# An adaLN block on one core: normalised rows of batches 2 and 3 turned by VectorE blocks and a DMA instead of TensorE

## The chip, the cores and the metric

The kernel runs on one core of a Trainium2 chip. The metric is the device time of one execution in microseconds (us). Engines are called PE (TensorE), DVE (VectorE), ACT (ScalarE), POOL (GpSimd) and SP (SyncE, which here only issues DMAs); PEld is the weight load of PE.

## The reference

Inputs are x (4 batches x 512 tokens x 512 features, fp32), a conditioning row c per batch, and weights. Cut to what matters:

```python
mod = (silu(c) @ wmod).reshape(4, 6, 1, 512)          # sa, ca, ga, sb, cb, gb
ga, gb = sign(g) * max(|g|, 0.25)                      # both gates
h = layernorm(x) * (1 + ca) + sa
qkv = h @ Wqkv + bqkv                                  # 512 -> 3 x 128
attn = softmax(q @ k.T / sqrt(128)) @ v
x = x + ga * (attn @ Wo + bo)
h = layernorm(x) * (1 + cb) + sb
logits = h @ gate_w.T + expert_bias                    # 4 experts, the best one counts
ffn = h @ W_up.T + (h @ A[e].T) @ B[e].T               # rank 8
out = x + gb * ffn
```

## The kernel before

All of x stays in SBUF (`xs`, 128 partitions = tokens of a tile, 4 batches x 4 tiles x 512). Every fp32 product is made of three products of a high and a low part (`products`, L344): `h1hi`/`h1lo`, `phi`/`plo`, `h2hi`/`h2lo` and so on. Each engine has an order written out by hand; semaphores counted per batch and tile tie the orders together, and no scheduler moves anything. PSUM's eight banks are given out by a list in order (`psum_plan`), and whoever opens a bank waits until its former holder is emptied.

A batch b goes through these steps. Layer norm 1: DVE statistics (`ln1_stats`, `ln1_moments`), POOL `ln1_deviation` and `ln1_offset` (1/std and shift), then ACT `ln1_normalise(b)` writes `xn1`, tokens on partitions. The projection needs features on partitions, so PE `x1_transposes(b)` turns 16 blocks of 128x128 into four banks; ACT `h1_high` evacuates them times (1 + ca), rounded, into `h1hi`; DVE `h1_low` makes `h1lo`. PE `qkv(b)` in two halves, `scores`, then DVE `maxima` and ACT `softmax`, PE `p_transposes`, ACT `pt_high` and DVE `pt_low`, PE `pv`, ACT `o_high` and DVE `o_low`, PE `out_projection`, DVE `residual` and `ln2_moments`, POOL `ln2_deviation`, ACT `ln2_normalise`, PE `x2_transposes`, ACT `h2_high` and DVE `h2_low`, and last the feed-forward products `up(b, t)` of 12 matmuls each, which PE runs between the attention steps of batch b + 1. DVE `gate_ffn` and POOL `outputs` finish a tile, SP stores it.

Names for the steps below: the loop `for b in range(1, B)` on every engine handles attention of batch b and the feed-forward part of b - 1. In it PE runs `x1_transposes(b + 1)` in the middle of `up(b - 1, 0)`. POOL runs `add_output_bias(b)`, then `output_weights(b + 1)` (L1379), which waits for `ga_bc`, a gate row of the next batch spread over the partitions, then `output_bias`, `ln1_deviation(b + 2)`, `ln1_offset(b + 2)` and `ln2_deviation(b, ...)` with `outputs(b - 1, ...)` between. SP issues in this order: `write_gate(1)` (waits for the gate rows "gb", which DVE's `gate_rows_evacuate` writes), the two spreads of gb, then the spread of `ga_bc` for batch 2, then the stores.

Of the kernel before, what the change touches and what calls it, by code (L numbers as in the profile page):

```python
# [11 lines left out]
P = 128  # L12
B = 4
# [12 lines left out]
BY_ACT = 3  # L26

# [16 lines left out]
def psum_plan():  # L44
# [43 lines left out]
def adaln_block(nc: bass.Bass, x, wqkv, bqkv, wo, bo, wup, gate_w, expert_bias, lora_a, lora_b, c, wmod, out):  # L88
    place, earlier = psum_plan()
    with ExitStack() as ctx:  # L90
# [3 lines left out]
        def sem(name):  # L94
# [11 lines left out]
        c_row = sb("c_row", [B, H])  # L106
# [58 lines left out]
        fb_hi = stage[:, 0, :]  # L165
# [21 lines left out]
        gates_out = sem("gates_out")  # L187
        stored = sem("stored")
# [10 lines left out]
            ln1_stats ln1_aggr ln1_var ln1_rstd ln1_shift xn1_ready xn1_by_act x1T_psum h1_hi h1_lo  # L199
# [57 lines left out]
        def _(sp):  # L257
# [25 lines left out]
            sp.dma_start(c_row[:], c).then_inc(c_in, 16)  # L283
# [48 lines left out]
        def _(pe):  # L332
# [296 lines left out]
            for kt in range(NK):  # L629
                mm = nc.tensor.transpose(dst[:, B * kt:B * kt + B], c_row[:, kt * P:(kt + 1) * P], ident[0:B, 0:B])  # L630
# [44 lines left out]
            for b in range(1, B):  # L675
# [60 lines left out]
        def _(act):  # L736
            def h1_high(b, kts=range(NK)):
                for kt in kts:
                    act.wait_ge(S["x1T_psum"], NK * b + kt + 1)
                    if b == 0 and kt % 2 == 0:  # L740
                        act.wait_ge(S["modT_ready"], 1 + kt // 2)
                    if b and kt == 0:
                        act.wait_ge(S["qkv_psum"], 3 * b)
# [172 lines left out]
            ln1_normalise(2)  # L916
            for b in range(1, B):
# [35 lines left out]
        def _(dve):  # L953
# [163 lines left out]
            def v_low(b):  # L1117
# [3 lines left out]
                                        ALU.subtract).then_inc(S["v_lo_ready"], 1)  # L1121

# [170 lines left out]
            for b in range(1, B):  # L1293
# [15 lines left out]
                if b + 2 < B:  # L1309
                    ln1_stats(b + 2, (0, 1, 2, 3))  # L1310
                    ln1_moments(b + 2)
                o_low(b)
                if not last:
# [7 lines left out]
                    qk_low(b + 1)  # L1321
                else:
# [25 lines left out]
        def _(pool):  # L1348
            def ln1_deviation(b):
# [95 lines left out]
            for b in range(1, B):  # L1445
# [8 lines left out]
                if not last:  # L1454
                    ln2_deviation(b, (0, 1))
# [32 lines left out]
```

## Time and profile before

| what | us |
|---|---|
| median of 3 runs (lowest to highest) | 194.16 (193.78 to 194.17) |
| the profiled execution, its own time | 194.07 |
| its span, first to last instruction | 192.2 |
| PE busy in the span | 177.0 (92%) |
| DVE, ACT, POOL busy | 137.6, 90.9, 79.5 |

The span is 1.9 us shorter than the execution's time. Times in rows count from the start of the span. Busy time of matmuls overlaps: a matmul of 512 columns is shown as some 0.39 us, but one starts every 0.23 us.

### The profile page before, as it was taken

Reading aid. Unit: us, or ns where it says so; the run is one execution under the profiler, and the core shown is the slowest. Engines: PE = TensorE matmul, PEld = TensorE weight load, DVE = VectorE, ACT = ScalarE, POOL = GpSimd, SP = SyncE. Lnnn points to the kernel's source line nnn. Section 1 sums busy time; section 2 is a strip of 40 time slices with the busy share of each in tenths; the row PEclk is TensorE's granted clock in tenths of the full one; section 3 lists DMA queues with packets and bytes.
Section 4 is the critical chain, followed back from the end, with each engine's and each line's share of the span. In section 5 each row is a group of like instructions: output and inputs, shape, how many; then the busy total and the mean of one; then the engine's idle time right before and its main releaser. Section 6 shows DMA issues by size and latency. Waiting matters only on the chain.

```text
span 192.2 us, 2846 instructions
## 1 busy us (share of the span) xinstructions
PE 177.0 (92%) x951; PEld 139.0 (72%) x951; DVE 137.6 (72%) x339; ACT 90.9 (47%) x172; POOL 79.5 (41%) x106
## 2 busy tenths in 40 slices
PE   6897999989998789986999999999999999988991
PEld 6874757866766658864888788878887887767770
DVE  1839748799989854796885478569566493986964
ACT  3355045954168976420746596113565622456110
POOL 3544200278154980005778940015696000332750
PEclk9999999999999999999999999999999999999999
DMA  5999996910033000022021500000232000001315
GB/s 173 381 385 386 382 269 108 398 64 5 0 79 141 3 2 0 0 76 95 0 109 55 164 3 0 0 0 3 109 122 42 3 0 3 0 0 55 144 42 196
DMA packets 12221, 19.21 MB, mean 100 GB/s; under 512 B 2812, under 2 KB 3328, under 8 KB 12208
## 3 DMA queue, kind: packets, MB, share of 16 engines
q1 hardware_dynamic: 12208, 19.05, 29.2%
q8 instruction: 7, 0.11, 0.2%
q14 instruction: 6, 0.05, 0.1%
HBM read 14.83 MB, written 4.21 MB: 99 GB/s over the span
## 4 chain that ended last, share of the span: by engine, by line
PE 45%; DVE 4%; issue 1%; ACT 1%; POOL 1%; DVEq 0%; POOLq 0%
PE bank L349 31%; PE bank L476 2%; PE bank L503 2%; PE bank L579 1%; DVE xs L1152 1%; DVE stats L1159 1%; PE bank L527 1%; PE bank L529 1%; PE bank L461 1%; PE bank L455 1%; PE bank L458 1%; PE bank L432 1%; PE bank L557 1%; DVE f_gb L1217 1%; ACT h2hi L844 1%
## 5 line engine op out<-in xcount | busy, mean ns | idle before, releaser
L1402 POOL TENSOR_TENSOR rstd<-var_eps,neg_half 128x1 f32<-128x1 f32 x16 | 8.8, 553 | 47.3 <-DVE var_eps L1163 47.3
L349 PE MATMUL bank<-wup_lo,h2hi 128*128 128x512 f32 x64 | 26.7, 417 | 0.6 <-DVE lbw L1085 0.6
L825 ACT ACTIVATE xn_p<-xs,shift,rstd 128x512 f32<-128x512 f32 x16 | 12.9, 815 | 27.7 <-POOL shift L1405 27.7
L349 PE MATMUL bank<-wup_hi,h2hi 128*128 128x512 f32 x64 | 25.3, 395 | 0.0
L349 PE MATMUL bank<-wup_hi,h2lo 128*128 128x512 f32 x64 | 25.2, 393 | 0.0
L1417 POOL TENSOR_TENSOR xs<-xs,f_gb 128x512 f32<-128x512 f32 x14 | 17.9, 1292 | 7.2 <-DVE f_gb L1217 7.2
L349 PE MATMUL bank<-h1lo,wqkv_hi 128*128 128x512 f32 x48 | 19.7, 411 | 1.2 <-ACT wqkv_hi L818 1.2
L1394 POOL TENSOR_TENSOR xs<-xs,gabo 128x512 f32<-128x512 f32 x16 | 20.3, 1302 | 0.1
L349 PE MATMUL bank<-h1hi,wqkv_hi 128*128 128x512 f32 x48 | 19.0, 395 | 0.0
L349 PE MATMUL bank<-h1hi,wqkv_lo 128*128 128x512 f32 x48 | 18.9, 394 | 0.0
L1379 POOL TENSOR_TENSOR wo_ga<-wo_raw,ga_bc 128x512 f32<-128x512 f32 x4 | 5.1, 1280 | 32.2 <-DMA ga_bc<-gates_dram 17.3
L1152 DVE SCALAR_TENSOR_TENSOR xs<-bank,row_inv,xs 128x512 f32<-128x512 f32 x16 | 12.0, 747 | 4.0 <-PE bank L349 2.6
L1126 DVE TENSOR_REDUCE row_max<-bank 128x1 f32<-128x512 f32 x16 | 10.9, 684 | 4.8 <-PE bank L461 4.8
L349 PEld LDWEIGHTS bank<-wup_lo,h2hi 128*128 128x128 f32 x64 | 12.1, 188 | 3.0 <-DVE lbw L1085 1.0
L349 PEld LDWEIGHTS bank<-wup_hi,h2hi 128*128 128x128 f32 x64 | 12.0, 188 | 2.8
L349 PEld LDWEIGHTS bank<-wup_hi,h2lo 128*128 128x128 f32 x64 | 12.1, 189 | 2.0
L1091 DVE SCALAR_TENSOR_TENSOR h1lo<-bank,modT_ca,h1hi 128x512 fp32r<-128x512 f32 x16 | 11.1, 742 | 3.4 <-ACT h1hi L744 3.3
L1135 DVE TENSOR_TENSOR plo<-bank,phi 128x512 fp32r<-128x512 f32 x16 | 10.0, 685 | 3.5 <-ACT phi L796 3.5
L961 DVE BATCH_NORM_STATS2 stats<-xs 128x6 f32<-128x512 f32 x16 | 10.2, 679 | 3.2 <-DMA xs<-in_L_attn_x_dram 3.2
L788 ACT ACTIVATE xn_p<-bank,neg_max 128x512 f32<-128x512 f32 x16 | 11.0, 686 | 3.0 <-DVE neg_max L1128 3.0
L1217 DVE TENSOR_TENSOR f_gb<-bank,gb_bc 128x512 f32<-128x512 f32 x16 | 10.6, 687 | 2.3 <-PE bank L579 2.1
L349 PEld LDWEIGHTS bank<-h1lo,wqkv_hi 128*128 128x128 f32 x48 | 9.0, 188 | 4.0 <-ACT wqkv_hi L818 1.4
(180 smaller groups left out, 421.7 us busy)
## 6 DMA issues: line engine op xcount, KB each, us to landing
out_dram<-xs SPq DMA_DIRECT2D x16, 256.0 KB, 2.0
stage<-in_L_wmod_dram SPq DMA_DIRECT2D x3, 1024.0 KB, 6.8
xs<-in_L_wmod_dram SPq DMA_DIRECT2D x3, 1024.0 KB, 9.0
xs<-in_L_attn_x_dram SPq DMA_DIRECT2D x3, 1024.0 KB, 6.7
xs<-in_L_attn_x_dram SPq DMA_DIRECT2D x2, 512.0 KB, 3.9
f_gb<-in_L_ffn_W_up_dram SPq DMA_DIRECT2D x1, 1024.0 KB, 10.5
gb_bc<-gates_dram SPq DMA_DIRECT2D x4, 256.0 KB, 3.6
xn_p<-in_L_attn_Wqkv_dram SPq DMA_DIRECT2D x4, 192.0 KB, 7.9
```

The source lines that it names most:

```text
L349: mm = nc.tensor.matmul(dst, w, m, start=first and i == 0, stop=last and i == total - 1)
L788: nc.scalar.activation(xn2_p[:, t, :], at("S", b, t)[:], ACT.Exp, bias=neg_max[:, t:t + 1], scale=SCORE_SCALE, accum_out=row_sum[:, t:t + ...
L825: nc.scalar.activation(xn2_p[:, t, :], xs[:, b, t, :], ACT.Identity, bias=shift[:, 1, t:t + 1], scale=rstd[:, 1, t:t + 1]).then_inc(S["xn2 ...
L961: nc.vector.bn_stats(stats[:, 0, t, :], xs[:, b, t, :]).then_inc(S["ln1_stats"], 1)
L1091: nc.vector.scalar_tensor_tensor(h1lo[:, kt, :], at("x1T", b, kt)[:], modT["ca"][:, kt, b:b + 1], h1hi[:, kt, :].bitcast(F32), ALU.mult, A ...
L1126: nc.vector.reduce_max(row_max[:, t:t + 1], at("S", b, t)[:], AX_X).then_inc(S["max_ready"], 1)
L1135: nc.vector.tensor_tensor(plo[:, :, q], at("PT", b, t)[:].rearrange("p (k q) -> p k q", k=NT), phi[:, :, q].bitcast(F32), ALU.subtract).th ...
L1152: nc.vector.scalar_tensor_tensor(xs[:, b, t, :], at("Y", b, t)[:], row_inv[:, t:t + 1], xs[:, b, t, :], ALU.mult, ALU.add).then_inc(S["x2_ ...
L1217: nc.vector.tensor_tensor(f_gb[:, n % 4, :], at("F", b, t)[:], gb_bc[:, b % 2, :], ALU.mult).then_inc(S["f_gb_ready"], 1)
L1394: nc.gpsimd.tensor_tensor(xs[:, b, t, :], xs[:, b, t, :], gabo[:], ALU.add).then_inc(S["xb_ready"], 1)
L1402: nc.gpsimd.tensor_tensor(rstd[:, 1, t:t + 1], var_eps[:, 1, t:t + 1], neg_half[:, 0:1], ALU.pow).then_inc(S["ln2_rstd"], 1)
L1417: nc.gpsimd.tensor_tensor(xs[:, b, t, :], xs[:, b, t, :], f_gb[:, n % 4, :], ALU.add).then_inc(S["out_ready"], 1)
```

## The change

For batches 2 and 3 PE no longer turns the normalised rows. ACT writes `xn1` in blocks of 32 features; DVE turns every 32x32 block in place (`turn_blocks`, four instructions); SP moves 16 pieces of 32 partitions x 2 KB from `xn1` to `stage` (`move_turned`), so that features stand on partitions; ACT scales them in place by (1 + ca) (`x1_scale`, four instructions) and rounds them into `h1hi` (`h1_high`, four); POOL makes `h1lo` (`h1_low`, four). The orders of all engines are written anew around that. `fb_hi` moves from `stage` to `c_rows`, and the banks of `fb` and `gzb` are exchanged. `NB` is 4, `BLOCK` 32, `TURNED` 2.

```diff
 # SP
+def move_turned(b):
+    sp.wait_ge(S["xn1_turned"], NT * (b - TURNED + 1))
+    if b > max(TURNED, 2):
+        sp.wait_ge(S["h1_lo"], NK * b)
+    for a in range(NB):
+        for c in range(NB):
+            sp.dma_start(turned_in[b][a * BLOCK:(a + 1) * BLOCK, c],
+                         xn1_blocks[c * BLOCK:(c + 1) * BLOCK, a]).then_inc(turned_moved, 16)
 ...
+            move_turned(2)
             write_gate(1)
 ...
                 if b + 2 < B:
                     spread_gate(0, b + 2)
+                if b == 1:
+                    move_turned(3)
 # PE
-                if last:
-                    up(b - 1, 0)
-                else:
-                    up(b - 1, 0, (0, 1))
-                    x1_transposes(b + 1)
-                    up(b - 1, 0, (2, 3))
+                up(b - 1, 0)
                 z_to_tokens(b - 1)
+                up(b - 1, 1, (0,))
                 p_transposes(b)
-                up(b - 1, 1)
+                up(b - 1, 1, (1, 2, 3))
 # ACT
+def x1_scale(b):
+    act.wait_ge(turned_moved, 16 * NB * NB * (b - TURNED + 1))
+    for kt in range(NK):
+        nc.scalar.activation(turned_in[b][:, :, kt], turned_in[b][:, :, kt], ACT.Copy,
+                             scale=modT["ca"][:, kt, b:b + 1]).then_inc(S["x1_scaled"], 1)
 ...
-            ln1_normalise(2)
             for b in range(1, B):
 ...
                 if b == 1:
+                    ln1_normalise(2)
+                    gz_evacuate(0)
 ...
+                if b == 2:
+                    x1_scale(3)
+                pt_high(b)
+                if b == 1:
+                    x1_scale(2)
                 if not last:
                     h1_high(b + 1)
-                pt_high(b)
                 o_high(b)
 # DVE
+def turn_blocks(b):
+    for t in range(NT):
+        xn1_done(dve, b, t + 1)
+        nc.vector.transpose(xn1_blocks[:, :, :, t], xn1_blocks[:, :, :, t]).then_inc(S["xn1_turned"], 1)
 ...
                 if b == 1:
+                    gate_shift()
+                    turn_blocks(2)
                     ffn_shift_rows()
-                    gate_shift()
-                if not last:
-                    h1_low(b + 1)
+                    ln1_stats(3, (0, 1, 2, 3))
+                    ln1_moments(3)
+                pt_low(b)
                 if b == 1:
                     gate_columns("gb")
-                pt_low(b)
+                choose_expert(b - 1)
                 if b == 1:
                     gate_rows_evacuate("gb")
-                choose_expert(b - 1)
                 inverse_sums(b)
-                if b + 2 < B:
-                    ln1_stats(b + 2, (0, 1, 2, 3))
-                    ln1_moments(b + 2)
                 o_low(b)
 ...
                     qk_low(b + 1)
+                    if b == 1:
+                        turn_blocks(3)
 # POOL
+def h1_low(b):
+    for kt in range(NK):
+        pool.wait_ge(S["h1_hi"], NK * b + kt + 1)
+        nc.gpsimd.tensor_tensor(by_blocks(h1lo[:, kt, :]), turned_columns(b, kt),
+                                by_blocks(h1hi[:, kt, :].bitcast(F32)), ALU.subtract).then_inc(S["h1_lo"], 1)
 ...
                     ln1_offset(b + 2)
                 if not last:
+                    h1_low(b + 1)
                     ln2_deviation(b, (0, 1))
```

Where POOL's order stood in pass b = 1 of the loop before (`wo_ga` is `output_weights(2)`, `var_eps` to `rstd` of 128x1 is `ln2_deviation`):

```order
L1379 TENSOR_TENSOR wo_ga<-wo_raw,ga_bc 128x512 [waits wo_lo_ready,wo_hi_ready,ga_bc_in0]
L1384 TENSOR_TENSOR gabo<-bo_bc,ga_bc 128x512 [waits xb_ready]
L1351 TENSOR_TENSOR rstd<-var_eps,neg_half 128x4 [waits ln1_var]
L1367 TENSOR_SCALAR shift<-moments,rstd 128x1 [waits ln1_rstd]
L1367 TENSOR_SCALAR shift<-moments,rstd 128x1 x3
L1402 TENSOR_TENSOR rstd<-var_eps,neg_half 128x1 [waits xn2_ready,ln2_var]
```

And the same place now:

```order
L1443 TENSOR_TENSOR wo_ga<-wo_raw,ga_bc 128x512 [waits wo_lo_ready,wo_hi_ready,ga_bc_in0]
L1448 TENSOR_TENSOR gabo<-bo_bc,ga_bc 128x512 [waits xb_ready]
L1415 TENSOR_TENSOR rstd<-var_eps,neg_half 128x4 [waits ln1_var]
L1431 TENSOR_SCALAR shift<-moments,rstd 128x1 [waits ln1_rstd]
L1431 TENSOR_SCALAR shift<-moments,rstd 128x1 x3
L1410 TENSOR_TENSOR h1lo<-stage,h1hi 128x512 [waits h1_hi] x4
L1466 TENSOR_TENSOR rstd<-var_eps,neg_half 128x1 [waits xn2_ready,ln2_var]
```

Four subtractions that DVE did before now stand on POOL between the shifts of layer norm 1 and the deviations of layer norm 2.

ACT's order now, pass b = 2, after the scores of batch 2 (`phi` is `pt_high(2)`, `stage` is `x1_scale(3)`, `h1hi` is `h1_high(3)`):

```order
L832 ACTIVATE xn_p,row_sum<-bank,neg_max 128x512 [waits negmax_ready]
L788 ACTIVATE stage<-stage,modT_ca 128x4x128 [waits turned_moved]
L788 ACTIVATE stage<-stage,modT_ca 128x4x128 x3
L840 ACTIVATE phi<-bank 128x4x128 [waits O_psum,PT_psum]
L840 ACTIVATE phi<-bank 128x4x128 [waits PT_psum] x3
L776 ACTIVATE h1hi<-stage 128x512 [waits x1_scaled,qkv_psum]
```

The wait for the 16 DMAs of batch 3 stands ahead of `pt_high(2)`; before, `h1_high(3)` stood there, and it waited for PE.

## Rows read from the trace of the kernel before

**Rows 1.** The page, part 1: busy time of each engine.
```profile
PE 177.0 (92%) x951; PEld 139.0 (72%) x951; DVE 137.6 (72%) x339; ACT 90.9 (47%) x172; POOL 79.5 (41%) x106
```

**Rows 2.** Timeline of PE: start, us, engine, line, op, count, [idle before].
```profile
73.30 1.91 PE L432 MATMUL bank<-ident,xn 128*128 128x128 f32 x16
74.97 0.47 PE L349 MATMUL bank<-wup_lo,h2hi 128*128 128x512 f32 x1
...
89.02 0.47 PE L349 MATMUL bank<-wo_lo,o_hi 128*128 128x512 f32 x1 [1.76 <-DVE o_lo L1144]
...
101.18 1.91 PE L503 MATMUL bank<-ident,xn_p 128*128 128x128 f32 x16
...
121.45 0.39 PE L349 MATMUL bank<-plo,v_hi 128*128 128x512 f32 x1
```

**Rows 3.** Timeline of POOL, end of the prelude and pass b = 1.
```profile
66.13 5.06 POOL L1394 TENSOR_TENSOR xs<-xs,gabo 128x512 f32<-128x512 f32 x4
88.53 1.28 POOL L1379 TENSOR_TENSOR wo_ga<-wo_raw,ga_bc 128x512 f32<-128x512 f32 x1 [17.34 <-DMA ga_bc<-gates_dram]
...
93.07 0.56 POOL L1402 TENSOR_TENSOR rstd<-var_eps,neg_half 128x1 f32<-128x1 f32 x1
...
97.01 0.55 POOL L1402 TENSOR_TENSOR rstd<-var_eps,neg_half 128x1 f32<-128x1 f32 x1
97.89 1.29 POOL L1417 TENSOR_TENSOR xs<-xs,f_gb 128x512 f32<-128x512 f32 x1
```

**Rows 4.** Timeline of ACT.
```profile
64.26 2.93 ACT L813 ACTIVATE xn<-xs,shift,rstd 128x512 f32<-128x512 f32 x4
...
69.55 0.68 ACT L788 ACTIVATE xn_p<-bank,neg_max 128x512 f32<-128x512 f32 x1
...
100.09 0.82 ACT L825 ACTIVATE xn_p<-xs,shift,rstd 128x512 f32<-128x512 f32 x1 [1.31 <-POOL shift L1405]
...
117.54 2.07 ACT L796 ACTIVATE phi<-bank 128x512 fp32r<-128x512 f32 x4 [0.96 <-PE bank L476]
```

**Rows 5.** Timeline of DVE.
```profile
77.96 2.48 DVE L1135 TENSOR_TENSOR plo<-bank,phi 128x512 fp32r<-128x512 f32 x4
81.87 0.68 DVE L1059 COPY gates<-bank 4x512 f32<-4x512 f32 x1 [1.43 <-PE bank L386]
...
85.09 2.44 DVE L961 BATCH_NORM_STATS2 stats<-xs 128x6 f32<-128x512 f32 x4
...
87.92 0.68 DVE L1144 TENSOR_TENSOR o_lo<-bank,o_hi 128x512 fp32r<-128x512 f32 x1
...
106.63 1.46 DVE L1113 SCALAR_TENSOR_TENSOR qk_lo<-bank,qb,qk_hi 128x512 fp32r<-128x512 f32 x2 [1.36 <-ACT qk_hi L766]
```

**Rows 6.** Groups by line: us busy, mean ns of one.
```profile
L1274 DVE COPY xn<-lora_b_raw 128x128 f32<-128x128 f32 x3 | 3.7, 1295 | 0.0
...
L851 ACT ACTIVATE wo_hi<-wo_ga 128x512 fp32r<-128x512 f32 x4 | 2.5, 630 | 0.4 <-POOL wo_ga L1379 0.4
```

**Rows 7.** Line L326, the stores: ns min/median/max of an issue; us to landing.
```profile
L326 SPq DMA_DIRECT2D out_dram<-xs x16: 332/332/338, 97.1 to 189.8; - x16
...
DMA to landing us min/median/max: 2.0/2.0/2.1
```

**Rows 8.** Line L281, the gate spreads, the same view.
```profile
DMA to landing us min/median/max: 3.1/3.6/3.9
```

**Rows 9.** Windows: stretch, length, busy of PE, PEld, DVE, ACT, POOL; granted clock; DMA.
```profile
190.00:191.60 1.60, 0.00 (x0) 0.00 (x0) 0.00 (x0) 0.00 (x0) 0.00 (x0) 1.00 0.45 168
191.60:192.20 0.60, 0.00 (x0) 0.00 (x0) 0.00 (x0) 0.00 (x0) 0.00 (x0) 0.55 0.00 0
```

**Rows 10.** Timeline of PE: its first matmuls and its last.
```profile
4.09 3.58 PE L335 MATMUL bank<-ident 128*128 128x128 f32 x16
...
13.44 1.06 PE L335 MATMUL bank<-ident 128*128 128x128 f32 x8
...
187.52 0.40 PE L579 MATMUL bank<-lbw,zT 128*128 128x512 f32 x1
```

More of the change, by code:

```diff
@@ L26 @@
 BY_ACT = 3
+TURNED = 2
+BLOCK = 32
+NB = P // BLOCK
 QUARTER = 32
@@ L57, in psum_plan @@
         (7, "x2T", 0, 0), (4, "x2T", 0, 1), (6, "x2T", 0, 2), (5, "x2T", 0, 3),
-        (2, "fb"), (7, "gzb"), (4, "gz", 0),
+        (7, "fb"), (2, "gzb"), (4, "gz", 0),
     ]
@@ L66, in psum_plan @@
         order += [(f[0], "F", b - 1, 0)]
-        if not last:
-            order += [(m[kt], "x1T", b + 1, kt) for kt in range(NK)]
         order += [(m[4], "zl", b - 1)] + [(m[t], "PT", b, t) for t in range(NT)] + [(f[1], "F", b - 1, 1)]
@@ L105, in adaln_block @@
         gz_bias = sb("gz_bias", [2 * GZ, B])
-        c_row = sb("c_row", [B, H])
+        c_rows = sb("c_rows", [P, H])
         silu_tmp = sb("silu_tmp", [P, 3, NK * B])
@@ L164, in adaln_block @@
         lora_b_rep = xn1[:, 0, 0:NK * ZROWS].rearrange("p (k a z) -> p k a z", k=NK, a=3)
-        fb_hi = stage[:, 0, :]
+        fb_hi = c_rows
+        xn1_blocks = xn1[:].rearrange("p t h -> p (t h)").rearrange("p (a k t i) -> p a k t i", a=NB, k=NK, t=NT)
+        turned_in = {b: (stage if b > 1 else h2lo)[:].bitcast(F32).rearrange("p t h -> p (t h)").rearrange(
+            "p (c k t i) -> p c k t i", c=NB, k=NK, t=NT) for b in range(TURNED, B)}
         mod_rows = gb_bc
@@ L187, in adaln_block @@
         gates_out = sem("gates_out")
+        turned_moved = sem("turned_moved")
         stored = sem("stored")
@@ L237, in tiles_of, with turned_columns, by_blocks, xn1_free @@
             return range(2 * half[0], 2 * half[0] + 2) if half else range(NT)
+        def turned_columns(b, kt):
+            return turned_in[b][:, :, kt].rearrange("p c t i -> p t c i")
+        def by_blocks(columns):
+            return columns.rearrange("p (t c i) -> p t c i", t=NT, c=NB)
+        def xn1_free(engine, b):
+            if b <= TURNED:
+                engine.wait_ge(S["x1T_psum"], NK * b)
+            else:
+                engine.wait_ge(turned_moved, 16 * NB * NB * (b - TURNED))
         def xn1_done(engine, b, t=NT):
@@ L629, in _ @@
             for kt in range(NK):
-                mm = nc.tensor.transpose(dst[:, B * kt:B * kt + B], c_row[:, kt * P:(kt + 1) * P], ident[0:B, 0:B])
+                mm = nc.tensor.transpose(dst[:, B * kt:B * kt + B], c_rows[0:B, kt * P:(kt + 1) * P], ident[0:B, 0:B])
             mm.then_inc(S["cT_psum"], 1)
@@ L738, in h1_high @@
                 for kt in kts:
+                    if b and kt == 0:
+                        act.wait_ge(S["qkv_psum"], 3 * b)
+                    if b >= TURNED:
+                        act.wait_ge(S["x1_scaled"], NK * (b - TURNED) + kt + 1)
+                        nc.scalar.activation(by_blocks(h1hi[:, kt, :]), turned_columns(b, kt),
+                                             ACT.Copy).then_inc(S["h1_hi"], 1)
+                        continue
                     act.wait_ge(S["x1T_psum"], NK * b + kt + 1)
@@ L809, in ln1_normalise @@
                     if t == 0:
-                        act.wait_ge(S["x1T_psum"], NK * b)
+                        xn1_free(act, b)
                         if b == 2:
                             act.wait_ge(S["loraB_psum"], 1)
-                    nc.scalar.activation(xn1[:, t, :], xs[:, b, t, :], ACT.Identity, bias=shift[:, 0, t:t + 1],
+                    nc.scalar.activation(xn1_blocks[:, :, :, t].rearrange("p a k i -> p k a i"),
+                                         xs[:, b, t, :].rearrange("p (k a i) -> p k a i", k=NK, a=NB), ACT.Identity, bias=shift[:, 0, t:t + 1],
                                          scale=rstd[:, 0, t:t + 1]).then_inc(S["xn1_by_act"], 1)
@@ L1090, in h1_low @@
                     dve.wait_ge(S["h1_hi"], NK * b + kt + 1)
+                    if b >= TURNED:
+                        nc.vector.tensor_tensor(by_blocks(h1lo[:, kt, :]), turned_columns(b, kt),
+                                                by_blocks(h1hi[:, kt, :].bitcast(F32)), ALU.subtract).then_inc(S["h1_lo"], 1)
+                        continue
                     nc.vector.scalar_tensor_tensor(h1lo[:, kt, :], at("x1T", b, kt)[:], modT["ca"][:, kt, b:b + 1],
@@ L1321, in _ @@
                     qk_low(b + 1)
+                    if b == 1:
+                        turn_blocks(3)
                 else:
```

12 lines of the change are left out of this document (4 added, 8 removed).

## The prediction

> **What bounds the kernel now.** I read the page first: PE is busy 92% of the span [rows 1]. Then PE's timeline: one matmul of 512 columns starts every 0.23 us almost without a gap, so in the middle of the program PE is the bound, and work taken from it counts in full only as long as nothing else becomes the last to arrive. So I read, for the two passes that change (attention of batch 1 and of batch 2), when each other engine delivers. The reader is to see two things. First, PE reaches `x2_transposes(1)` at 101.18 [rows 2], and ACT's last normalised tile for it, begun at 100.09, ends at 100.91 [rows 4]: there is 0.27 us of slack, and behind that tile stands a chain of POOL that starts at 88.53, when the gate row `ga_bc` of batch 2 has landed [rows 3]. POOL is 41% busy over the span, yet here it is as late as PE. Second, PE reaches `pv(2)` at 121.45 [rows 2], 20.27 after 101.18; that is all the room that ACT and DVE have there; ACT's last part for it is ready at 119.61 (117.54 + 2.07) [rows 4], DVE's 0.7 later.
>
> **What the change takes from PE.** Two times 16 transposes. The next matmul starts 1.67 us after the first of them [rows 2], so 3.3 us in all. In pass 1 it also takes away most of the largest wait, 1.76 us for `o_lo` [rows 2]: DVE ran the statistics of batch 3 just before it (85.09 to 87.92) [rows 5], and these now stand ahead of `pt_low(1)`. With all of this PE would end some 5 us earlier. The rest is whether it can.
>
> **Pass 1, the gate row.** SP issues the spread of `ga_bc` behind `write_gate(1)`, which waits for DVE's copy of the gate rows "gb". I follow DVE.
> - ACT's normalisation of batch 2 (2.93 us) [rows 4] now stands behind `softmax(1)`. Softmax ended at 70.23 (69.55 + 0.68) [rows 4]; without the normalisation ahead of it I take it 0.8 earlier, paced by the maxima: 69.4. Normalisation ends at 72.4.
> - DVE turns tile by tile behind it. No row shows a block transpose. Nearest are plain passes over 512 columns at 0.61 us each (2.44 for four) [rows 5]; above, the slowest SBUF copy took 1.3 us [rows 6]. Below 0.61 nothing is gained here, since ACT delivers a tile only every 0.7. I take 0.61 to 0.65: the last ends at 73.05.
> - ACT evacuates `gz` and `fb`, two copies of 0.6 like its other copies [rows 6], to 73.6; `ffn_shift_rows`, a pass of 0.7 with a semaphore on either side, to 74.4; statistics and moments of batch 3, 2.83 [rows 5], to 77.25; `pt_low(1)`, 2.48 [rows 5], to 79.75. It began at 77.96 before and begins 0.7 earlier now.
> - `gate_columns`, four tiny instructions, 0.65 as an estimate, then `choose_expert(0)`, 2.5 (between the copy's end and 85.09) [rows 5], which now stands ahead of the copy; the copy 0.68 [rows 5]. It ends at 83.7, against 82.55 (81.87 + 0.68) before.
> - From the copy's end to POOL's start two DMAs and their issues take 88.53 - 82.55 = 5.98 [rows 3, 5]. So POOL starts `output_weights(2)` at 89.7, 1.15 later than before. The 16 DMAs of batch 2, issued ahead of `write_gate(1)` from 73.1 on, are done by then (below).
>
> **Pass 1, POOL.** `output_weights(2)` to `ln1_offset(3)`: 93.07 - 88.53 = 4.54 [rows 3], to 94.24. Then the four subtractions of `h1_low(2)`: a two-input pass of POOL costs 5.06 us for four, one every 1.25 [rows 3], so 5.0, to 99.25. Before, DVE did them and POOL was already waited for. Then `ln2_deviation(1)` for four tiles at 0.88 each, with two `outputs` at 1.25 between (97.01 to 97.89, and 1.29 overlapped) [rows 3]: 6.05, to 105.3. ACT's normalisation 0.82 [rows 4], and 0.14 to PE: `x2_transposes(1)` starts at 106.3 against 101.18, **5.1 us late**. PE has nothing else to run: `qkv(2)`'s first half waits for the first two `h1_low` parts (95.5 and 96.8) and is over at 99.7, so PE stands still for about 6.6 us. All gains of pass 1, the transposes and the `o_lo` wait, fall into this gap. Whatever holds `o_high(1)` back behind the scaling on ACT falls into it too, up to some 5 us.
>
> **The clock in that gap.** PE's granted clock stays at 2.4 GHz through the longest wait of the middle, 1.76 us. After its last matmul (over at 187.92) [rows 10] it holds to 191.6 and is lower in the next window, a mean of 0.55 of full, which means 1.2 GHz [rows 9]: 3.7 us of rest were enough there, and 6.6 are expected here. I take it to fall. What that costs: the 16 warm-up matmuls at the program's start came one every 0.21 us ((3.58 - 0.4) / 15), eight of the same kind at 13.44 one every 0.11 [rows 10]. So each us of work at the low level loses half of itself. At the start at least these 3.58 us ran at the low level, a loss of 1.8, and twice as long would be 3.6. Taken: 2.5; zero if the clock holds.
> The Trainium skill, "TensorE: Matmul & The Clock Gate", HAM oscillation, has the rule that a long enough gap between bursts throttles PE again and the next burst begins cold. The end of this trace agrees; by the rule the sum has the 2.5, without it it has not.
>
> **Pass 2, the DMAs.** Count from x2_transposes(1), called X. DVE ends `qk_low(2)` at X + 6.9 (106.63 + 1.46) [rows 5]. `turn_blocks(3)` follows with 4 x 0.6, to X + 9.3. SP issues 16 DMAs: an issue takes 0.332 [rows 7] and the next follows 0.04 later, so 15 x 0.37 = 5.6, and the last lands 2.0 after its issue as a store does [rows 7]: X + 16.9. Bounds: 0.3 a piece and, since no row shows a landing in SBUF from SBUF, three quarters of the store's 2.0 (6.0 in all); 0.5 a piece and 3.6 as a gate spread [rows 8] (11.1); taken 7.6, since stores are plain copies issued by the same engine. ACT has x1_scale(3) **ahead of** `pt_high(2)`: 4 x 0.6 (0.630 for a copy from SBUF [rows 6]) to X + 19.3, `pt_high` 2.07 [rows 4] to X + 21.4, DVE's last `pt_low` 0.7 later: pv(2) starts at X + 22.1, against X + 20.27 before: **1.9 us late**, with bounds 0.3 and 5.4. PE's saving of pass 2, 1.67, is lost in this wait as well. Behind it `h1_high(3)` (2.2) and `o_high(2)` fit under pv's 2.8, and POOL's `h1_low(3)` (5.0, from X + 22 on) ends before the first deviation of batch 2 is asked for at about X + 29. From there on the rest of the program is as before; pass 3 only gets `p_transposes` 0.7 later in PE's order, with 2.1 us of matmuls between them and `pv(3)` for ACT and DVE.
>
> **The sum.** 194.07 + 5.1 + 2.5 + 1.9 = **203.6 us**. That is against the profiled execution; its time lies 0.09 under the median of 194.16, which I leave out.
>
> **The rivals.**
> - The clock holds at 2.4 GHz in the gap (the activity before it or the phase saves it): 201.1. Against it stands only the end of this trace. 20%.
> - DVE's block transposes are slow, 1.3 us each. For it: the copies of `xn1` from SBUF took that beside POOL's work [rows 6]. Pass 1 then ends the turning at 70.1 + 5.2 = 75.3 rather than 73.05 and `ffn_shift_rows` at 76.1 rather than 74.4, so +1.7; in pass 2 +2.8: 208.1. Against it: these copies had pieces of 32 columns at odd places and ran beside POOL, which waits in pass 1. 12%. The Trainium skill, "VectorE: DVE Perf Modes", The three transpose paths, gives 311 ns for 128 columns of bf16; an estimate of four times that is 1.24 us for 512, which would make this rival's time by the page. No row here shows it.
> - The DMAs are slow as at the upper bound, or PE's second gap (3.5 us before pv(2)) lets the clock fall a second time: 206 to 207. 13%.
> - PE stays the bound, because POOL gets `ga_bc` and finishes `h1_low(2)` early. Place: POOL's chain to `ln2_deviation(1)`. It decides if POOL reaches this by 94 rather than 99.25; then PE is never held, and 194.07 - 3.3 - 1.8 = 189 us, faster. For it: POOL is idle from 71.2 to 88.53. Against it: it is idle because it waits for `ga_bc` (17.34) [rows 3], the change puts `choose_expert(0)` ahead of that copy, and POOL's order is fixed. 4%; half-way cases that end near before, 3%.
> The forecast itself has the remaining 48%.
>
> **Range and chances.** Low end: clock holds and the DMAs at their lower bound, 194.07 + 5.1 + 0.3 = 199.5. High end: forecast with slow transposes or the DMAs' upper bound, 208. What is left out below and above is about 2 in 10. A difference under 0.2% (0.4 us) can't be told from none here. Faster 0.05, same 0.02, slower 0.93.
>
> **What would show it.** In the profile after: POOL's `wo_ga` starts near 89.7, its four `h1lo` rows follow at 94.2 with 1.25 each, PE's `x2` transposes of batch 1 start near 106.3 with an idle of about 6 us before them released by ACT's normalisation, and matmuls behind it come at 0.43 us for some 5 us. PE waits 3 to 4 us before pv(2), released by DVE `plo`, behind ACT `stage` waiting for a DMA. The chain that ended last goes through POOL and through 16 SBUF-to-SBUF DMAs. Wrong would be: `wo_ga` before 88, `h1lo` rows well under 1 us, or no idle of PE before x2 of batch 1. The four bn_stats of batch 3 ahead of `pt_low(1)` should leave no `o_lo` wait of DVE's making.

## The result and the profile after

The changed kernel takes **208.31 us** (median of 4 runs, 207.67 to 208.68) against 194.08 for the kernel before on the same chip: ratio 1.0732, 95% interval 1.0703 to 1.0762. The direction was right; the time lies 4.7 above the forecast and 0.3 above the range. The profiled run took 208.41, its span 206.7, 14.5 more than before.

The page, part 1 and one row of part 2, then one row of part 4 (the chain that ended last, by line):

```profile
PE 178.8 (86%) x919; PEld 139.2 (67%) x919; DVE 138.8 (67%) x339; ACT 95.5 (46%) x180; POOL 89.4 (43%) x114
...
PEclk9999999999999999976999998569999999999999
...
PE bank L386 25%; SPq L314 9%; POOL h1lo L1410 2%; DVE xn L1179 2%; PE bank L540 2%; DMA ga_bc<-gates_dram 2%; POOL rstd L1466 2%; DVE qk_lo L1166 1%; DVE h2lo L1151 1%; POOL xs L1481 1%; DVE plo L1193 1%; DVE xs L1210 1%; DVE stats L1217 1%; PE bank L498 1%; DMA stage<-xn 1%
```

PE issues 32 matmuls fewer than in [rows 1] and is still busy 1.8 us longer. The two dips of its clock row account for it: the 21 matmuls of 512 columns in them are shown as 0.63 us instead of 0.39. And a queue that before was no part of the chain, SP issuing the pieces (L314), is now 9% of it. PE's timeline, to be held against [rows 2]:

```profile
91.25 0.77 PE L386 MATMUL bank<-wo_lo,o_hi 128*128 128x512 f32 x1 [5.48 <-DVE o_lo L1202]
91.81 0.63 PE L386 MATMUL bank<-wo_hi,o_lo 128*128 128x512 f32 x1
...
106.35 1.97 PE L540 MATMUL bank<-ident,xn_p 128*128 128x128 f32 x16 [0.24 <-ACT xn_p L870]
...
133.82 0.76 PE L386 MATMUL bank<-plo,v_hi 128*128 128x512 f32 x1 [8.62 <-DVE plo L1193]
134.38 0.63 PE L386 MATMUL bank<-phi,v_lo 128*128 128x512 f32 x1
```

PE stands still twice: 5.48 us before `out_projection(1)`, where it had waited 1.76, and 8.62 before `pv(2)`, where it had not waited. X, the start of `x2_transposes(1)`, is at 106.35 instead of 101.18 (+5.17), and `pv(2)` at X + 27.47 instead of X + 20.27 (+7.20). Behind both gaps a matmul of 512 columns is followed by the next after 0.43 us instead of 0.23. Windows (stretch, length, busy of PE, PEld, DVE, ACT, POOL, granted clock, share and GB/s of the DMA engines) show why:

```profile
86.00:91.00 5.00, 0.00 (x0) 0.00 (x0) 0.69 (x1) 4.75 (x9) 1.06 (x1) 0.90 0.44 157
91.00:97.00 6.00, 5.75 (x14) 4.61 (x15) 1.78 (x4) 2.93 (x4) 5.90 (x10) 0.51 0.01 3
97.00:106.00 9.00, 9.00 (x40) 7.04 (x38) 7.57 (x16) 2.96 (x4) 8.06 (x12) 1.00 0.14 52
...
125.00:127.00 2.00, 0.21 (x1) 0.00 (x0) 0.00 (x0) 0.00 (x0) 0.00 (x0) 1.00 0.43 103
127.00:134.00 7.00, 0.18 (x1) 0.21 (x2) 2.81 (x5) 5.88 (x11) 0.79 (x1) 0.54 0.04 10
134.00:138.00 4.00, 4.00 (x10) 3.13 (x11) 2.47 (x12) 0.68 (x2) 4.00 (x4) 0.52 0.00 0
138.00:150.00 12.00, 12.00 (x55) 9.64 (x55) 8.61 (x18) 3.50 (x5) 4.68 (x9) 1.00 0.06 22
```

PE rests, the clock falls to 1.2 GHz during the rest, and it stays there for the first stretch of work behind it (0.51 and 0.52 of full). In the first rest it falls only near the end (a mean of 0.90 from 86 to 91), in the second early (0.54 from 127 on). The other engines (ACT, then POOL, then SP's queue, then DVE's new operation):

```profile
85.15 2.56 ACT L788 ACTIVATE stage<-stage,modT_ca 128x512 f32<-128x512 f32 x4 [7.26 <-DMA stage<-xn]
87.62 2.17 ACT L776 ACTIVATE h1hi<-stage 128x512 fp32r<-128x512 f32 x4
89.69 0.57 ACT L848 ACTIVATE o_hi<-bank 128x512 fp32r<-128x512 f32 x1
...
128.12 2.56 ACT L788 ACTIVATE stage<-stage,modT_ca 128x512 f32<-128x512 f32 x4 [8.09 <-DMA stage<-xn]
130.58 2.03 ACT L840 ACTIVATE phi<-bank 128x512 fp32r<-128x512 f32 x4
```

```profile
89.94 1.27 POOL L1443 TENSOR_TENSOR wo_ga<-wo_raw,ga_bc 128x512 f32<-128x512 f32 x1 [18.81 <-DMA ga_bc<-gates_dram]
...
94.44 4.99 POOL L1410 TENSOR_TENSOR h1lo<-stage,h1hi 128x512 fp32r<-128x512 f32 x4
...
105.19 0.27 POOL L1469 TENSOR_SCALAR shift<-moments,rstd 128x1 f32<-128x1 f32 x1
```

```profile
73.57 10.10 SPq L314 DMA_DIRECT2D stage<-xn  x16
...
115.76 10.89 SPq L314 DMA_DIRECT2D stage<-xn  x16
```

```profile
71.07 2.47 DVE L1179 STREAM_TRANSPOSE xn<-xn 128x512 f32<-128x512 f32 x4
```

Read together: DVE's turning costs 0.62 us a tile, as taken. Sixteen DMAs take SP 10.1 us to issue, and the data is ready for ACT at 85.15, 11.6 us after the last tile was turned (73.54). ACT's `o_high(1)` stands behind scaling and `h1_high(2)`, so it begins at 89.69 and PE waits for its low part. POOL, busy without a break from 89.94 to 105.46, arrives at x2_transposes(1) at the same time as PE. Its chain isn't independent of the pieces either. From the view of the chain that ended last (start, us, what), the last of batch 2's pieces, the write of the gate rows right behind it, and one piece of batch 3:

```profile
83.08 0.59 SPq L314
83.72 1.62 DMA gates_dram<-gates
...
122.02 1.46 SPq L314
```

`write_gate(1)` had to wait for DVE's copy of the gate rows, which ended at 83.55 (82.88 + 0.67), and for SP, which was busy with the pieces until 83.67. The two ends lie 0.1 us apart.

### The profile page after: what moved, and what is told of

It reads as the page before. It is cut to its first block, busy times and chain, and to the rows that moved or that the text cites. A ratio compares the mean times of both kernels' runs of the same rounds, so it can differ in the third digit from the quotient of the medians.

```text
span 206.7 us, 2829 instructions
## 1 busy us (share of the span) xinstructions
PE 178.8 (86%) x919; PEld 139.2 (67%) x919; DVE 138.8 (67%) x339; ACT 95.5 (46%) x180; POOL 89.4 (43%) x114
## 4 chain that ended last, share of the span: by engine, by line
PE 37%; DVE 12%; SPq 10%; POOL 8%; DMA 4%; issue 3%; ACT 3%; POOLq 0%; DVEq 0%
PE bank L386 25%; SPq L314 9%; POOL h1lo L1410 2%; DVE xn L1179 2%; PE bank L540 2%; DMA ga_bc<-gates_dram 2%; POOL rstd L1466 2%; DVE qk_lo L1166 1%; DVE h2lo L1151 1%; POOL xs L1481 1%; DVE plo L1193 1%; DVE xs L1210 1%; DVE stats L1217 1%; PE bank L498 1%; DMA stage<-xn 1%
## 5 line engine op out<-in xcount | busy, mean ns | idle before, releaser
L1410 POOL TENSOR_TENSOR h1lo<-stage,h1hi 128x512 fp32r<-128x512 f32 x8 | 10.0, 1280 | 14.5 <-ACT h1hi L776 14.5
L386 PE MATMUL bank<-plo,v_hi 128*128 128x512 f32 x16 | 7.4, 462 | 8.6 <-DVE plo L1193 8.6
L386 PE MATMUL bank<-wo_lo,o_hi 128*128 128x512 f32 x16 | 7.6, 476 | 6.0 <-DVE o_lo L1202 5.9
```

Of the source, the lines that this page charges most:

```text
L386: mm = nc.tensor.matmul(dst, w, m, start=first and i == 0, stop=last and i == total - 1)
L1410: nc.gpsimd.tensor_tensor(by_blocks(h1lo[:, kt, :]), turned_columns(b, kt), by_blocks(h1hi[:, kt, :].bitcast(F32)), ALU.subtract).then_inc ...
```

## The experiments

All times are medians. The kernel before was run beside them on the same chip each time: 193.69 (probe, few, low_dve, scale_late), 193.84 (warm, early, pool_half), 193.74 (warm32, best, moved) and 193.78 (best_sp). Beside the changed kernel it was 194.08, and the changed kernel itself was run only there, so a difference of two medians from different groups is uncertain by some 0.3 us. Times read from traces don't depend on that.

**probe: DMAs by themselves, behind the end of the kernel before.** One group of DMAs after another, with all engines idle; the group that copies as the change does, SBUF to SBUF, 32 partitions x 2 KB (L348 in its rows):

```diff
+for i in range(16):
+    sp.dma_start(probe_b[32 * (i // 4):32 * (i // 4) + 32, i % 4, :], probe_a[32 * (i % 4):32 * (i % 4) + 32, i // 4, :]).then_inc(probed, 16)
```

> The kernel before, with groups of DMAs issued by SP behind its last store, each group waited for: 16 stores of 128 partitions x 2 KB back to back; 16 stores of 32 partitions x 2 KB; 16 copies from SBUF to SBUF of 32 partitions x 2 KB, as the change makes them; 4 copies SBUF to SBUF of 128 partitions x 2 KB; 4 of 32 partitions x 8 KB; 4 of 32 partitions x 2 KB, each waited for before the next. It asks why an issue of the change takes 0.59 us where a store takes 0.33. Theory A, the form (SBUF at both ends): the third and the last groups show 0.59, both groups of stores 0.33. Theory B, back-to-back issue fills a queue: every group of 16 settles near 0.6 and the last group, issued alone, shows 0.33. Theory C, the number of partitions: groups with 32 partitions 0.59, those with 128 0.33. The time is some 40 to 60 us above the kernel before and means nothing by itself.

Rows of the view of one line (ns min/median/max of an issue, first and last start): 128-partition stores, 32-partition stores, pieces back to back, pieces each waited for:

```profile
L340 SPq DMA_DIRECT2D probe_dram<-wup_hi x16: 326/642/652, 191.6 to 200.9; - x16
```
```profile
L344 SPq DMA_DIRECT2D probe_dram<-wup_hi x16: 302/426/437, 204.0 to 211.2; - x16
```
```profile
L348 SPq DMA_DIRECT2D stage<-wup_hi x16: 586/591/617, 212.9 to 222.5; - x16
```
```profile
L360 SPq DMA_DIRECT2D stage<-wup_hi x4: 507/507/508, 236.1 to 242.0; - x4
```

The price follows both from the form and from the company. A store of 128 partitions takes 332 ns where stores come one by one [rows 7], and 326 as the first of the probe's group; the same store behind others takes 642. A store of 32 partitions behind others is 426, a copy of 32 partitions into SBUF 591, or 507 when each is waited for. One piece follows the other after (222.5 - 212.9) / 15 = 0.64 us on a quiet chip, as in the changed kernel. So the engines and the other DMAs that ran beside the pieces in the changed kernel don't make them slow. Two groups more had bigger copies into SBUF: 602 ns an issue and 2.5 us to landing for 128 partitions x 2 KB, 662 ns and 4.3 us for 32 partitions x 8 KB. Four issues of the second kind carry the bytes of sixteen pieces; no run here tries to merge the pieces into so few.

**few: 4 of the 16 pieces of each batch** (the other 12 blocks are not moved, so what ACT scales is partly old data; the work behind it is the same).

```diff
-                    for c in range(NB):
+                    for c in (a,):
 ...
```

> The changed kernel, but only 4 of the 16 pieces of each batch are moved (those with equal indices); the other 12 are left out, so batches 2 and 3 are computed from stale columns. Theory: SP's serial issue is what made pass 2 late. The move shrinks from 12.4 us to 4 x 0.63 + 2.0 = 4.5; ACT's scaling of batch 3 then starts at 120.3 instead of 128.1, pv(2) at 125.6 instead of 133.8, and PE's clock does not fall there: 208.3 - 8.2 - 1.9 = 198.2 us. In pass 1 the start of x2_transposes(1), 106.35, stays, as POOL's chain sets it. Rival, the landing of a copy into SBUF is what is slow and not its issue: 4 pieces take nearly as long as 16, 206 or more. Rival, both passes shrink: 193 or less.

Measured: **201.69** (ratio 1.0415, 1.0398 to 1.0433), 6.6 less than the changed kernel, 3.5 more than expected. PE's rows:

```profile
96.92 0.47 PE L386 MATMUL bank<-h1lo,wqkv_hi 128*128 128x512 f32 x1 [3.34 <-issue]
...
107.39 3.67 PE L540 MATMUL bank<-ident,xn_p 128*128 128x128 f32 x16 [4.50 <-ACT xn_p L870]
...
128.74 0.47 PE L386 MATMUL bank<-plo,v_hi 128*128 128x512 f32 x1 [0.42 <-DVE plo L1193]
```

The waits for `o_lo(1)` and before `pv(2)` are gone: both were the pieces. But X did not move forward: PE now rests before `qkv(2)`, which needs POOL's `h1_low(2)` (from 95.55 on), and again before x2_transposes(1), 7.8 us in all. That is what the prediction had said of POOL's chain, with 6.6. In the second rest the clock falls and what follows is slow (3.67 us for 16 transposes instead of 1.97), which is on the path this time. PE is through with its work ahead of `pv(2)` 20.9 us after X, in `early` (below), at full clock, 18.75, so this fall costs 2.2. X came 1.0 later than in the changed kernel since ga_bc(2) reached POOL at 91.00 rather than 89.94. These two make up most of the 3.5.

**low_dve: h1_low(2) and (3) by DVE, ahead of o_low, instead of POOL.**

```diff
                 inverse_sums(b)
+                if not last:
+                    h1_low(b + 1)
                 o_low(b)
 ...
                 if not last:
-                    h1_low(b + 1)
                     ln2_deviation(b, (0, 1))
```

> The changed kernel with the low parts of batches 2 and 3 made by VectorE again (ahead of o_low) instead of GpSimd; GpSimd's 5.0 us between the shifts of layer norm 1 and the deviations of layer norm 2 are gone. Theory of the prediction: GpSimd's chain alone holds x2_transposes(1), which moves from 106.35 to 101.4: about 203.4 us. Rival, which the profile after suggests: PE itself reaches that place only 0.24 us earlier, because o_high(1) waited on ScalarE behind the 16 DMAs of batch 2 (5.5 us idle of PE and a fallen clock), so two chains of equal length end there and taking one away gives 0.3 us at most: 208.0 to 208.5.

Measured: **208.07** (ratio 1.0745, 1.0720 to 1.0770), no change. POOL lost 5 us of work and X is at 106.99. PE's wait for `o_lo(1)` grew to 6.93 us, since DVE had the four subtractions ahead of it. PE reaches X without a wait. So another chain stands where POOL's was taken away, but the run made that chain 1.45 us longer itself (`out_projection(1)` at 92.70 instead of 91.25); without that it would have ended near 105.5, an estimate. It doesn't separate the two chains; `few` and `best_sp` do.

**scale_late: x1_scale(3) behind pt_high(2).**

```diff
-                if b == 2:
-                    x1_scale(3)
                 pt_high(b)
                 if b == 1:
                     x1_scale(2)
+                if b == 2:
+                    x1_scale(3)
```

> The changed kernel with ScalarE's scaling of batch 3 behind pt_high(2) instead of ahead of it; nothing else. Theory: pv(2) no longer waits for the DMAs and starts at about 125.1, but o_high(2) stands behind scaling and rounding on ScalarE (128.1 + 4.7 = 132.9), so out_projection(2) starts at 134.1 instead of 140.3: 208.3 - 6.2 = 202.1 us if the clock falls in the 4.5 us gap, 200.3 if it holds. Rival, the order on ScalarE does not matter since the DMA must land in any case before qkv(3): 208.

Measured: **204.27** (ratio 1.0543, 1.0516 to 1.0570). `pv(2)` starts at 125.07, without a wait. But the late pieces hold the next one, `o_high(2)`, and the clock falls here too (granted 0.80 in the mean from 134 to 142):

```profile
133.93 0.77 PE L386 MATMUL bank<-wo_lo,o_hi 128*128 128x512 f32 x1 [4.05 <-DVE o_lo L1202]
```

Half of the late wait goes, half moves on: this order on ACT doesn't hide pieces that land 12 us after the turning. The time is 2.2 above the 202.1 expected, although `out_projection(2)` began when expected (133.93 against 134.1): the expectation had counted the slow stretch behind `pv(2)` as saved and set nothing against it for the new slow stretch behind `out_projection(2)`.

**warm and warm32: matmuls that nobody reads, in PE's gap before pv(2).**

```diff
+                if b == 2:
+                    keep_warm(open_bank("F", b - 1, 2), 64)
                 pv(b)
```

> The changed kernel with 64 matmuls of 128 columns more, that nobody reads, between PE's last up-projection part and pv(2), where PE otherwise stands still for 8.6 us (some 6.8 us of work at 0.107 each). Theory (the second fall of the granted clock costs time of its own): PE enters pv(2) at 2.4 GHz, its matmuls come every 0.23 us instead of 0.43, and the time falls by 1.8 to 2.0 us, to 206.4. Rival (what follows pv(2) is held by ACT and DVE anyway, so that the slow matmuls are hidden): 208.3, no change. pv(2) itself starts at 133.8 by both.

Measured: **212.06** (ratio 1.0943, 1.0926 to 1.0959). I had mis-sized the filling: 64 of these matmuls are 128 passes and last 14.45 us, so `pv(2)` began at 139.03, 5.2 later, while the time grew by only 3.75. With half of them:

> As warm, with half the filling: 32 matmuls, which are 64 passes on TensorE (warm's 64 were 128 passes and took 14.45 us, 5.2 more than the gap has), so 7.2 us of the gap of 9.0. pv(2) starts at 133.8 as in the changed kernel, now at 2.4 GHz. Theory (the second fall of the clock costs time of its own): 206.4. Rival (hidden): 208.3.

Measured: **206.79** (ratio 1.0666, 1.0650 to 1.0682), 1.5 less than the changed kernel, though PE does 7.3 us more work:

```profile
124.32 7.31 PE L372 MATMUL bank<-ident 128*128 128x128 f32 x64
...
133.07 0.47 PE L386 MATMUL bank<-plo,v_hi 128*128 128x512 f32 x1 [1.44 <-DVE plo L1195]
```

`pv(2)` begins at full clock (0.47 instead of 0.76). In this profiled run it begins 0.75 earlier than in that of the changed kernel, and the runs stand at 206.07 and 208.41, so 2.3 - 0.75 = 1.6 us are the clock. (All of that trace lies 0.7 to 0.8 earlier from the turning on: the DVE instruction ahead of it took 0.37 us there and 1.63 in the changed kernel.) `warm` gives 5.2 - 3.75 = 1.5. The traces alone say the same: from `pv(2)` to x2_transposes(2) it is 18.63 us in the changed kernel and 16.94 in `warm32`, 1.7 less. So the second fall costs about 1.6 us.

**early: batch 3 turned ahead of h2_low(1), its pieces issued amid the stores of batch 0.** Nothing is removed.

```diff
+                    if b == 1:
+                        turn_blocks(3)
                     h2_low(b)
                     qk_low(b + 1)
-                    if b == 1:
-                        turn_blocks(3)
...
                 for t in range(NT):
+                    if b == 0 and t == 2:
+                        move_turned(3)
```

> The changed kernel with VectorE's turning of batch 3 ahead of h2_low(1), where DVE has 2.8 us to wait, and with its 16 DMAs issued in the middle of the stores of batch 0. Nothing is removed. Theory (what batch 3 costs is only that its DMAs start late, behind qk_low(2), and take 16 x 0.65 + 2): turning 105.0 to 107.5, last piece landed 119.3, x1_scale(3) behind softmax from 119.9, pt_low over at 125.3, pv(2) starts near 125.4, which is where PE itself arrives (X + 18.65 = 125.0); no gap, no second fall of the clock: 208.3 - 8.4 - 1.9 = 198.0. Rival (stores and pieces in one queue hold each other up: four stores of 256 KB beside 16 pieces of 64 KB, and ga_bc(3) some 7 us later): pieces ready no earlier than 123, pv(2) at 129: 202 to 203.

Measured: **198.38** (ratio 1.0241, 1.0215 to 1.0267). SP's queue and PE:

```profile
102.35 2.46 SPq L363 DMA_DIRECT2D out_dram<-xs  x2
107.32 10.02 SPq L314 DMA_DIRECT2D stage<-xn  x16
117.38 1.08 SPq L363 DMA_DIRECT2D out_dram<-xs  x2
```
```profile
124.93 0.47 PE L386 MATMUL bank<-plo,v_hi 128*128 128x512 f32 x1
```

`pv(2)` starts at 124.93 without a wait. The pieces cost as much as ever; they only began 8.4 us sooner. Two stores of batch 0 and the spread of ga_bc(3) came some 7 us later, and nobody on the path missed them.

**pool_half: 8 pieces issued by SP, 8 by GpSimd** (on a semaphore of its own, both waited for by ACT).

```diff
-            move_turned(2)
+            move_turned(sp, 2, (0, 1), turned_moved)
...
+                    move_turned(pool, b + 1, (2, 3), turned_by_pool)
```

> The changed kernel with the same 16 DMAs per batch, 8 of them issued by SP and 8 by GpSimd, on a semaphore of their own. Theory (the price is the issue of one engine, 0.63 to 0.68 us a piece): batch 2 is ready for ACT near 80.1 instead of 85.15 and the wait for o_lo(1) of 5.5 us goes, but X stays at 106.3 since POOL's chain sets it as well (with the clock falling in a gap there instead, + up to 1.5); batch 3 is ready at 122.8 instead of 128.1, pv(2) starts at 128.3: 208.3 - 5.5 - 1.9 = 200.9, up to 202.4. Rival 1 (the DMA engines, not the issue, set the pace of the pieces): ready at 85 and 128 as before, 208.3. Rival 2 (an issue of GpSimd costs 1 us or more): ready at 83 and 126, 205 to 206.

Measured: **206.16** (203.77 to 206.43; ratio 1.0597, 1.0533 to 1.0662). One of the four runs lies 2.3 us under the others; why stays open.

```profile
L283 SPq DMA_DIRECT2D stage<-xn x16: 523/591/649, 73.6 to 121.6; - x16
L283 POOL DMA_DIRECT2D stage<-xn x16: 496/496/704, 73.9 to 120.9; - x16
```
```profile
86.82 0.47 PE L388 MATMUL bank<-wo_lo,o_hi 128*128 128x512 f32 x1 [1.03 <-DVE o_lo L1205]
...
106.21 3.52 PE L542 MATMUL bank<-ident,xn_p 128*128 128x128 f32 x16 [6.06 <-ACT xn_p L873]
...
131.07 0.77 PE L388 MATMUL bank<-plo,v_hi 128*128 128x512 f32 x1 [4.48 <-DVE plo L1196]
```

The mechanism is as expected: the issue sets the pace, an issue of GpSimd costs 0.5 us, and batch 2 is ready for ACT at 80.71 instead of 85.15. The size is not: 2 us won instead of 6 to 7.5. The gap of pass 1 is where `few` had its longer one, before x2_transposes(1), with the slow stretch on the path, so that DVE turned batch 3 1.4 us later. Landing took up to 3.7 us (median 2.6) instead of 2.0 besides, and the pieces were ready at 125.36 rather than 122.8; then the clock fell again before `pv(2)`.

**best: the turning kept, the order around it changed.** GpSimd issues half of batch 2's pieces, batch 3 as in `early`, and further, in words rather than code:

```diff
 DVE  +gate_columns("gb")            (ahead of pt_low(1))
       pt_low(b)
      +gate_rows_evacuate("gb")      (ahead of choose_expert(0))
 POOL +ln1_deviation(3), ln1_offset(3), h1_low(2)   (ahead of output_weights(2), in the idle time)
 ACT   h1_high(b + 1, (0, 1)); o_high(b); h1_high(b + 1, (2, 3))
```

> All of the changed kernel's turning by DVE and DMAs, with another order around it: batch 2's pieces issued half by SP and half by GpSimd; batch 3 turned ahead of h2_low(1) and its pieces issued amid the stores; the gate columns ahead of pt_low(1) and the copy of the gate rows ahead of choose_expert(0); on POOL the deviation and offset of batch 3 and h1_low(2) ahead of output_weights(2); o_high between the halves of h1_high on ACT. Theory (two chains of equal length met at x2_transposes(1), POOL's and that through o_high; and the late pieces made the rest): pieces ready 80.7, h1_low(2) on POOL 83.8 to 89, ga_bc at 88, output_weights to 91.5, ln2_deviation(1) 6.05 to 97.5, X = 98.5 against 101.18 in the kernel before; pass 2 without a wait saves its 1.67: 194.07 - 2.7 - 1.7 = 189.7, faster than both. Rival (DVE's extra 5 us and ACT's extra 2.6 a batch are a bound of their own in these passes, or some PE gap lets the clock fall again): 193 to 196.

Measured: **190.42** (190.22 to 191.51; ratio 0.9837, 0.9816 to 0.9858), faster than both kernels, than the one before by 1.6%.

```profile
84.28 5.05 POOL L1415 TENSOR_TENSOR h1lo<-stage,h1hi 128x512 fp32r<-128x512 f32 x4 [4.06 <-ACT h1hi L778]
89.26 1.33 POOL L1448 TENSOR_TENSOR wo_ga<-wo_raw,ga_bc 128x512 f32<-128x512 f32 x1
```
```profile
86.18 0.47 PE L388 MATMUL bank<-wo_lo,o_hi 128*128 128x512 f32 x1 [0.36 <-DVE o_lo L1207]
...
98.77 1.97 PE L542 MATMUL bank<-ident,xn_p 128*128 128x128 f32 x16 [0.27 <-ACT xn_p L873]
```

X is at 98.77 (98.5 expected). POOL's four subtractions last as long as before; they only lie in the time in which it had waited for ga_bc.

**best_sp: best, but SP issues all 16 pieces of batch 2.** It puts the late `o_high` back, with POOL's short order kept.

> The reordered kernel `best`, but all 16 pieces of batch 2 are issued by SP again; POOL's chain keeps the shorter order it has there. Theory (PE's chain through the late pieces holds x2_transposes(1) by itself: pieces 85.15, four scalings 2.56, half of h1_high 1.1, o_high and o_low 1.4): out_projection(1) starts at 90.3, with the clock fallen in the gap before it, and X at 105.0 against 98.8 in best: 190.4 + 6.2 = 196.6. Rival (only POOL's chain held X, and the late o_high is hidden behind other work of PE): X at 99, 190.4 to 191.

Measured: **196.43** (ratio 1.0132, 1.0097 to 1.0167).

```profile
90.61 0.77 PE L386 MATMUL bank<-wo_lo,o_hi 128*128 128x512 f32 x1 [4.83 <-DVE o_lo L1204]
105.09 1.91 PE L540 MATMUL bank<-ident,xn_p 128*128 128x128 f32 x16
```

No wait at X, and X 6.3 us later than in `best`: PE's chain through the late pieces suffices by itself. (POOL is done with its last shift at 103.96, nearly as late, but it had stood 1.75 us waiting for the residual behind the late `out_projection(1)`, so that too comes from the pieces.) In `few` POOL's sufficed by itself. Alone, the one chain held X at 105.1 and the other at 107.4.

**moved: the kernel before, all transposes on PE, with the two moves of `best` that need no turning:** statistics of batch 3 ahead of h1_low(2) on DVE, its deviation and offset ahead of output_weights(2) on POOL.

> The kernel before, all transposes on PE, with the statistics and moments of batch 3 ahead of h1_low(2) on DVE, and its deviation and offset ahead of output_weights(2) on POOL. It shows how much the orders give without any turning. Theory (PE's wait of 1.76 us for o_lo(1) is DVE's statistics, and X then lies 1.7 earlier with POOL 2 us earlier too): X = 99.4, 192.3. Rival (another chain takes the wait over at once): 193.5 to 194.1.

Measured: **192.03** (191.92 to 192.31; ratio 0.9912, 0.9899 to 0.9926). X is at 99.04. Of the 3.3 us by which `best` beats the kernel before, half is had without turning. The two differ by 1.6, and `best` has moves that `moved` has not, so the turning's own worth is 1.6 at the most that these runs show, of the 3.3 that PE's transposes took.

## Why the prediction was wrong in size and right in kind

**Right, pass 1 by POOL.** The gate copy ended at 83.55 (83.7 predicted), `wo_ga` began at 89.94 (89.7), `h1_low` at 94.44 (94.24) with 1.25 us each, X at 106.35 (106.3). The transposes' savings on PE vanished as said, and `few` shows this chain alone sufficient. One premise of it held by luck. The prediction had the 16 DMAs of batch 2 done long before the gate copy's end; SP was busy with them until 83.67, 0.1 us behind that end, so an issue any slower would have moved POOL's chain and X as well. In `few`, where SP was free, `write_gate(1)` was issued at 83.52 instead of 83.72.

**Right, DVE's turning.** 0.62 us a tile, at the low end of the bounds taken; the rival with 1.3 us is excluded. The last tile was turned at 73.54 instead of 73.05, since the DVE instruction ahead of the turning took 1.6 us. The Trainium skill, "VectorE: DVE Perf Modes", The three transpose paths, gives 311 ns for a 128x128 tile of bf16; my estimate of 1.24 us from it for 512 columns is not borne out (659 to 702 ns an instruction), the measurement decides.

**Wrong, the step "SP issues 16 DMAs: an issue takes 0.332 [rows 7] and the next follows 0.04 later".** Measured: 0.59 an issue and 0.63 from one to the next; one issue of batch 3 took 1.46. Its last issue started 10.3 us after the first, and the data were in use at 128.12, 12.4 us after the turning was over. I had taken 7.6 and called 11.1 the upper bound. The landing, 2.0, was right. The row I took stood for another kind of DMA, with a pause ahead of each issue; `probe` shows that either difference matters. So ACT had the data at X + 21.8 and not at X + 16.9, **+4.9**, and with 0.5 more for scaling, `pt_high` and `pt_low` behind it (5.7 instead of 5.2) `pv(2)` came at X + 27.47 and not at X + 22.1. Against the kernel before it was 7.2 late instead of 1.9 (the prediction's own figures give 1.8): **+5.3**. `early` removes it all by starting 8.4 us sooner.

**Wrong, the second fall of the clock.** It stood among the rivals (13%) since the gap was put at 3.5 us; it was 8.6. The sum had nothing for what lies behind `pv(2)`. The transposes that follow it, x2_transposes(2), before and now:

```profile
138.12 1.91 PE L503 MATMUL bank<-ident,xn_p 128*128 128x128 f32 x16
```
```profile
152.45 1.91 PE L540 MATMUL bank<-ident,xn_p 128*128 128x128 f32 x16
```

They start 18.63 us behind `pv(2)` instead of 16.67, and 0.2 more is lost from there to the end: **+2.1**. Of this the clock is 1.6 to 1.7, since with full clock the stretch takes 16.94 in `warm32` and 17.01 in `early`. The other 0.3 of the stretch is there in these runs too, and no run looks into it. The Trainium skill's rule ("TensorE: Matmul & The Clock Gate", HAM oscillation) that a long enough gap throttles PE and the next burst begins cold agrees with this trace at both gaps (granted 0.51 and 0.52 behind them).

**Wrong, the place of the first gap.** The prediction had PE wait 6.6 us before x2_transposes(1) and put 2.5 us of slow work behind it. The late pieces held `o_high(1)`, and PE waited before `out_projection(1)` instead. The clock fell there, and the 12 matmuls behind it lost 2.4 us, but PE still reached X just when POOL did (0.24 us of wait), so this fall cost nothing: **-2.5**. I had named the cause ("Whatever holds `o_high(1)` back behind the scaling on ACT falls into it too, up to some 5 us") and drawn no conclusion for the clock, nor seen that it made a second chain of equal length. `few` and `pool_half` have a gap where I had put it, and there the fall does cost, 2.2 us in `few`.

**The sum with the terms as measured:** 203.6 + 0.1 for X + 5.3 + 2.1 - 2.5 = 208.6. The changed kernel's time is 1.7 us above its span and that of the kernel before 1.9, which takes off 0.2: 208.4, the profiled 208.41. The range's upper end took the DMAs' bound or the slow transposes, never a bound too low together with the second fall.

## What to carry to other kernels

Price a burst of DMAs by a burst of the same kind; a row of lone issues can be half of it. When a transfer takes 12 us, ask first how early it can start: of what these pieces cost, a move in the order gave back 10 us, twelve pieces fewer per batch 6.6. And where two engines reach a point within a fraction of a us of each other, shortening one shows nothing: find the second chain before you judge the first.

## What was not expected of the hardware

- The price of a DMA issue on SP depends on what precedes it: the 128-partition store takes 0.33 us alone and 0.64 behind others; the 32-partition copy into SBUF 0.51 and 0.59. GpSimd issues the same copy in 0.50.
- TensorE's granted clock fell during rests of 5.5 and 8.6 us; the work behind them ran at 1.2 GHz for 5.5 and 4.0 us. It fell at a rest of 4.05 us (`scale_late`) too. In `few` it fell behind a rest of 3.34 us, when PE had already been working again for 1.3 us (1.00 until 98.0, 0.50 from 98.5 to 101). In the kernel before it had kept 2.4 GHz through 1.76 (1.00 from 84 to 93). Useless matmuls in such a rest made the kernel 1.5 us faster.
- The same spread of ga_bc arrived 1.0 us later in `few` than in the changed kernel, although it was issued 0.4 us sooner. Its cause stays open.
- The DVE instruction ahead of the turning (L1128, 72x4 elements) takes 1.6 us in the traces of nine kernels with turning, 0.37 in that of `warm32` and 0.2 in those of the kernels without turning. That puts off the start of the turning by 1.2 us. Its cause stays open.
